# Routing a mixture of experts inside the attention before it, and streaming a later stage's logits

## The reference, cut to what matters

```python
t = t + _L2_attn_ref(_ln_t(t), Wq, Wk, Wv)            # causal attention, one head, 128 wide
t = t + _L2_ffn_ref(_ln_t(t), router_w, gate_w, up_w, down_w)
#   x = _ln_t(t);  router_logits = x @ router_w.T      # 16 experts
#   top_vals, top_idx = top_k(router_logits, 2);  weights = softmax(top_vals)
#   out = sum over the two of weights * ((silu(x @ gate) * (x @ up)) @ down)
...
t = t + _L3_ffn_ref(_ln_t(t), gate_weight, experts)
#   gate_logits = x @ gate_weight                      # 8 experts; then 8 rounds of Sinkhorn
```

## Time and profile before

| | |
|---|---|
| time, three runs | median 4058.59 us (4056.32 to 4060.82) |
| profiled execution | 4049.84 us, span 4048.0 us, mean granted TensorE clock 0.886 of full speed |
| busy: TensorE, VectorE, ScalarE, GpSimd | 83%, 76%, 46%, 27% of the span |
| attention | 1105 to 1332 us |
| routing | 1332 to 1560 us |
| logits of `sinkhorn_gates` | from 3789 us |

### The profile page before, as it was taken

How to read it: one execution, slowest core, us unless ns; L and a number is a source line. 1 busy time by engine, 2 the same in 40 slices (tenths; PEclk the granted TensorE clock), 3 DMA queues, 4 the chain that set the end, 5 groups by cost and what they waited for, 6 DMA issues and landing times. The chain is left out here.

```text
span 4048.0 us, 131348 instructions
## 1 busy us (share of the span) xinstructions
PE 3351.7 (83%) x54119; PEld 2132.4 (53%) x54119; DVE 3089.8 (76%) x7658; ACT 1857.2 (46%) x4392; POOL 1093.1 (27%) x1947
## 2 busy tenths in 40 slices
PE   5999999996699514996679999999679999998529
PEld 1333333222367412664357788877267788876414
DVE  7888788865766642556868999998868999997477
ACT  1666666673334101334456655554356655554200
POOL 1001001000000374551055544333056543332000
PEclk7999999998799656996579999999589999999659
DMA  6023233300000211224000000000000000000128
GB/s 145 24 48 54 39 54 54 54 8 6 0 1 1 87 51 50 67 69 156 1 9 15 9 9 9 9 4 6 4 8 15 9 9 9 9 4 9 47 74 302
DMA packets 102446, 155.92 MB, mean 39 GB/s; under 512 B 17060, under 2 KB 63017, under 8 KB 101824
## 3 DMA queue, kind: packets, MB, share of 16 engines
q1 hardware_dynamic: 87616, 120.28, 11.6%
q0 software_dynamic: 13088, 23.06, 2.0%
q10 hardware_dynamic: 1152, 4.19, 0.3%
HBM read 103.21 MB, written 45.30 MB: 37 GB/s over the span
## 5 line engine op out<-in xcount | busy, mean ns | idle before, releaser
L2079 ACT ACTIVATE s_E<-s_Y,s_M 128x9 f32<-128x9 f32 (+38 forms) x2048 | 656.6, 392 | 626.7 <-DVE s_M L1992 624.3
L365 DVE TENSOR_REDUCE half_max<-shared 128x1 f32<-128x512 f32 x1024 | 644.9, 684 | 89.0 <-PE shared L286 86.5
L1893 PE MATMUL g_x<-s_ik,s_iqm 128*32 128x1 f32 (+63 forms) x16384 | 676.4, 280 | 27.1 <-DVE g_o L1975 11.6
L482 ACT ACTIVATE E<-sc 128x1024 f32<-128x1024 f32 x512 | 496.7, 1021 | 268.8 <-PE sc L300 268.7
L1987 DVE SCALAR_TENSOR_TENSOR s_Y<-s_Y,g_x 128x9 f32<-128x9 f32 (+38 forms) x2048 | 578.7, 283 | 46.8 <-PE g_x L1893 1.2
L1905 PE MATMUL g_p<-mats,s_E 128*128 128x128 f32 x3072 | 448.1, 283 | 38.6 <-ACT s_E L2079 34.2
L1893 PEld LDWEIGHTS g_x<-s_ik,s_iqm 128*32 128x32 f32 x16384 | 395.1, 116 | 153.8 <-issue 79.4
L1905 PEld LDWEIGHTS g_p<-mats,s_E 128*128 128x128 f32 x3072 | 338.9, 144 | 104.4 <-ACT s_E L2079 60.4
L286 PE MATMUL shared<-ks,qs 96*128 96x512 bf16 x1024 | 373.5, 403 | 18.4 <-DVE half_max L365 13.3
L1992 DVE TENSOR_REDUCE s_M<-s_Y 128x4 f32<-128x8 f32 (+56 forms) x512 | 351.2, 686 | 0.8 <-DVE s_Y L1987 0.4
L2003 DVE TENSOR_TENSOR resid<-g_p,s_W 128x512 f32<-128x512 f32 x384 | 263.7, 687 | 59.7 <-PE g_p L1905 56.6
(11 more groups left out here) (353 smaller groups left out, 5227.2 us busy)
## 6 DMA issues: line engine op xcount, KB each, us to landing
e_spread<-d_gate SPq DMA_DIRECT2D x64, 512.0 KB, 6.1
d_parts<-parts SPq DMA_DIRECT2D x8, 1536.0 KB, 5.9
qs<-d_parts SPq DMA_DIRECT2D x96, 128.0 KB, 7.3
ks<-d_parts SPq DMA_DIRECT2D x96, 128.0 KB, 12.4
me_xg<-d_xs SPq DMA_DIRECT2D x144, 65.0 KB, 1.8
mc_yb<-d_ys SPq DMA_DIRECT2D x8, 1024.0 KB, 8.0
resid<-in_x SPq DMA_DIRECT2D x8, 512.0 KB, 8.2
rden<-d_den POOLq DMA_DIRECT2D x16, 256.0 KB, 3.7
```

The costliest lines, as they stand in the source:

```text
L365: dve.tensor_reduce(half_max[n // SETS % 2][:, idx // 2, idx % 2:idx % 2 + 1], bank("bm", n)[:, :], AX_X, ALU.max).then_inc(max_done, 1)
L482: act.activation(E[:, G % 2, h, :], sc[n % 2][:, :], ACT.Exp, scale=0.25).then_inc(exp_done, 1)
L1893: mm = pe.matmul(x_ps[u % 3][32 * b:32 * (b + 1), rho % 2, 0:n + 1], iqm[n // WINDOW % 2][:, b, x0:x0 + D, :], s.ik[:, b, rho, 0:n + 1], s ...
L2079: act.activation(E[:, m % 2, rho, 0:m + 1], Y[:, D * (m % YR) + rho, 1:2 + m], ACT.Exp, bias=M[:, D - 1 + D * m + rho:D + D * m + rho]).th ...
```

## The change

`layer2_attention` and `moe_route` become one block, `attend_and_route`. While batch r + 1 is attended, batch r is routed in pieces, each placed in a step; eight more steps without attention follow the 64 for batch 7.

- p0, p1 (`LOGITS`): TensorE makes the logits, half a batch each, straight from the residual; the router's weights are centred over the features once at the start, and since the deviation scales a token's 16 logits alike, the two best are the same. The difference of the best two is multiplied with 1/deviation later (`mark`).
- p1 (`BEST`): VectorE copies the logits out and takes the best.
- p2 and p4 (`FIRST`, `SECOND`): TensorE transposes half a batch in, VectorE takes the moments, ScalarE the root (Sqrt between the attention's Exp). In the steps behind them VectorE normalizes that half into `xt`.
- p3 (`INDEX`), p5 (`MARK`): VectorE's indices, then mask and running sum.
- p6 (`RANK`), p7 (`PLACE`): the two rank matmuls, then the positions. GpSimd scatters 16 times from there, as before.

The transposes back and ScalarE's copy of the normalized tokens are gone. Logits, transposed tokens and ranks share one PSUM bank; the even steps' scores get a half-size one. The weights' load starts with the attention; the zero rows are written by SP, with direct DMAs at 16 addresses loaded into registers, behind `padded`. The tables' large tensors lie in `t.xn`.

In `sinkhorn_gates` the gate's weights, padded to 32 columns, are the stationary operand and 512 tokens are streamed; four batches go to the four groups of 32 PSUM partitions. ScalarE and VectorE copy the rows out, 16 transposes bring the tokens back to the partitions, and the clip is done in two halves.

```diff
+                def logits(r, h):
+                    if h == 0:
+                        pe.wait_ge(added, NT * (r + 1))
+                        if r:
+                            pe.wait_ge(picked, r)
+                    for j in range(4 * h, 4 * h + 4):
+                        mm = pe.matmul(r_ps[:, j * NE:(j + 1) * NE], t.resid[:, r * T + j * P:r * T + (j + 1) * P],
+                                       centred[:, :], start=True, stop=True)
...
+                def tokens_in(r, h):
+                    if h == 0:
+                        pe.wait_ge(logit_done, r + 1)
+                    else:
+                        pe.wait_ge(normed, 2 * r + 1)
...
+                for g in range(STEPS + NT):
+                    r, p = g // NT - 1, g % NT
+                    if g < STEPS:
+                        turn(g, 0)
+                        if tile(g) >= HB:
+                            turn(g, 1)
+                        if g + 2 < STEPS:
+                            scores(g + 2)
+                        if piece(g):
+                            project(*piece(g))
+                    if r >= 0:
...
+                        if p in LOGITS:
+                            logits(r, p)
+                        if p == FIRST:
+                            tokens_in(r, 0)
+                        if p == SECOND:
+                            tokens_in(r, 1)
+                        if p == RANK:
+                            ranks(r)
+                    if g < STEPS:
+                        values(g)
...
+                    if r >= 0:
...
+                        if p == FIRST:
+                            moments(r, 0)
+                        if p == FIRST + 1:
+                            normalize(r, 0)
+                        if p == SECOND:
+                            moments(r, 1)
+                        if p == SECOND + 1:
+                            normalize(r, 1)
+                        if p == BEST:
+                            best(r)
+                        if p == INDEX:
+                            indices(r)
+                        if p == MARK:
+                            mark(r)
+                        if p == PLACE:
+                            place(r)
+                    if g < STEPS:
+                        finish(g)
...
+                for g in range(STEPS + NT):
+                    r, p = g // NT - 1, g % NT
+                    if g < STEPS:
+                        take_turned(g)
+                        if piece(g) and piece(g)[1] < 2:
+                            take_queries(*piece(g))
+                        if g + 2 < STEPS:
+                            exp(g + 2)
+                    if r >= 0 and p in (FIRST, SECOND):
+                        deviation(r, p == SECOND)
...
+                for r in range(2):
+                    for h in range(2):
+                        for q in range(4):
+                            c0 = (4 * r + q) * T + h * HALF
+                            mm_ = pe.matmul(rows_ps[32 * q:32 * q + 32, r, h * HALF:(h + 1) * HALF], f.gate_w[:, :],
+                                            t.xn[:, c0:c0 + HALF], start=True, stop=True)
```

More of the change, by code:

```diff
@@ new lines, in attend_and_route @@
+        logit = sb("logit", [P, NT, NE])
+        top = sb("top", [P, NT, 8])
+        index = sb("index", [P, NT, 8], U32)
+        indexf = [sb(f"indexf{i}", [P, 2, NT]) for i in range(2)]
+        gap = sb("gap", [P, NT])
+        diff = sb("diff", [P, B, NT])
+        mask = [sb(f"mask{i}", [P, NE, NQ + 1], BF16) for i in range(2)]
+        before = [sb(f"before{i}", [P, NE, NQ + 1], BF16) for i in range(2)]
+        chosen = sb("chosen", [P, NQ, NE])
+        rank = sb("rank", [P, NQ])
+        ones = sb("ones", [P, P], BF16)
@@ new lines, in attend_and_route @@
+        share = sb("share", [P, P])
+        centred = sb("centred", [P, NE])
+        lower = sb("lower", [P, P], BF16)
+        go_on = sb("go_on", [P, NE, NQ + 1], BF16)
+        iota_e = sb("iota_e", [P, NE])
+        iota_id = sb("iota_id", [P, NT])
+        iota_n = sb("iota_n", [P, TILES])
+        iota_r = sb("iota_r", [P, TILES])
+        iota_k = sb("iota_k", [P, N // P])
+        iota_pad = sb("iota_pad", [P, NE])
+        pad = sb("pad", [P, ROW])
+        count = sb("count", [P, NE])
@@ L926, in layer2_attention @@
+        pad_pos = sb("pad_pos", [P, NE], I32)
+        tiles = sb("tiles", [P, NE])
+        one_e = sb("one_e", [P, NE])
+        ends = sb("ends", [P, NE])
+        first = sb("first", [P, TILES])
+        full = t.xn[:, 0:NE * (N // P)].rearrange("p (e k) -> p e k", e=NE)
+        past = t.xn[:, T:T + TILES * NE].rearrange("p (n e) -> p n e", e=NE)
+        begun = t.xn[:, 4 * T:4 * T + TILES * NE].rearrange("p (n e) -> p n e", e=NE)
+        s_ps = [psum("s_ps0", HALF), psum("s_ps1", T)]
         t_ps = [psum(f"t_ps{i}", HALF) for i in range(2)]
+        x_ps = psum("x_ps", HALF)
@@ L1003, in values @@
                 def values(g):
[L1004 removed]
+                    b, n_tile = g // NT, tile(g)
                     if g % NT == 0:
@@ L1021, in _ @@
                 scores(1)
[L1022 to L1030, removed]
+                pe.wait_ge(m.router_in, 16)
+                pe.wait_ge(const, 4)
+                pe.matmul(r_ps[:, 0:NE], share[:, :], m.w_router[:, :], start=True, stop=True).then_inc(summed_w, 1)
+                for g in range(STEPS + NT):
[9 more added lines that the diff above has]
+                    if r >= 0:
+                        if r == 0 and p == 0:
+                            pe.wait_ge(centred_w, 1)
+                        if p in LOGITS:
[8 more added lines that the diff above has]
+                        values(g)
+                pe.wait_ge(picked, B)
+                pe.matmul(r_ps[:, 0:NE], ones[:, :], before[(B - 1) % 2][:, :, NQ], start=True, stop=True).then_inc(mm_n, 1)
             @block.vector
@@ L1059, in finish, with moments @@
                     dve.wait_ge(mm_o, g + 1)
-                    r = t.resid[:, c0:c0 + P]
-                    dve.tensor_tensor(r, o_ps[:, :], r, ALU.add).then_inc(added, 1)
+                    x = t.resid[:, c0:c0 + P]
+                    dve.tensor_tensor(x, o_ps[:, :], x, ALU.add).then_inc(added, 1)
+                def moments(r, h):
+                    k = 2 * r + h
+                    dve.wait_ge(token_in, k + 1)
+                    for j in range(4 * h, 4 * h + 4):
+                        bn = dve.bn_stats(stats[:, j, :], in_ps[:, (j - 4 * h) * P:(j - 4 * h + 1) * P])
+                    bn.then_inc(stat, 1)
+                    dve.wait_ge(stat, 2 * k + 1)
+                    if k:
+                        dve.wait_ge(root, k)
+                    for j in range(4 * h, 4 * h + 4):
+                        bn = dve.bn_aggr(mv[:, j, :], stats[:, j, :])
+                    bn.then_inc(stat, 1)
@@ new lines, in normalize @@
+                def normalize(r, h):
+                    k, i, four = 2 * r + h, r % RING, slice(4 * h, 4 * h + 4)
+                    dve.wait_ge(root, k + 1)
+                    dve.reciprocal(rstd[:, four], std[:, four]).then_inc(recip, 1)
+                    dve.wait_ge(recip, k + 1)
+                    if r >= RING:
+                        dve.wait_ge(sent[i], 16 * NQ * (r // RING))
+                    for j in range(4 * h, 4 * h + 4):
+                        ts = dve.tensor_scalar(xt[i][:, j, 0:P], in_ps[:, (j - 4 * h) * P:(j - 4 * h + 1) * P],
+                                               mv[:, j, 0:1], rstd[:, j:j + 1], ALU.subtract, ALU.mult)
+                    ts.then_inc(normed, 1)
@@ L1068, in _ @@
                 topmost(1)
-                scale(0)
-                for g in range(STEPS):
-                    if tile(g) >= HB:
-                        take_turned(g)
-                    if g + 1 < STEPS:
-                        scale(g + 1)
-                    if g + 2 < STEPS:
-                        topmost(g + 2)
-                    if piece(g) and piece(g)[1] >= 2:
-                        take_values(*piece(g))
-                    finish(g)
+                dve.wait_ge(summed_w, 1)
@@ new lines, in _ @@
+                dve.wait_ge(mm_n, 1)
+                dve.tensor_copy(count[:, :], r_ps[:, 0:NE]).then_inc(table, 1)
+                dve.wait_ge(table, 1)
+                dve.tensor_tensor(pad_pos[:, :], count[:, :], iota_pad[:, :], ALU.add).then_inc(padded, 1)
+                dve.tensor_tensor(full, count[:, :].unsqueeze(2).to_broadcast([P, NE, N // P]),
+                                  iota_k[:, :].unsqueeze(1).to_broadcast([P, NE, N // P]), ALU.is_gt).then_inc(table, 1)
+                dve.wait_ge(table, 2)
@@ new lines, in _ @@
+                dve.tensor_reduce(tiles[:, :], full, AX_X, ALU.add).then_inc(table, 1)
+                dve.wait_ge(table, 3)
+                dve.tensor_tensor_scan(ends[:, :], one_e[:, :], tiles[:, :], 0.0, ALU.mult, ALU.add).then_inc(table, 1)
+                dve.wait_ge(table, 4)
```

(16 more changed lines are left out.)

509 lines of the change are left out of this document (201 added, 308 removed).

## The result

The changed kernel took 3887.96 us (median of 4 runs, 3876.72 to 3893.91) beside 4057.45 us for the kernel before in the same session (4 runs, 4048.74 to 4060.82): a ratio of 0.9587, 95% interval [0.9561, 0.9612]. The forecast was 3918 in a range of 3880 to 3960. The profiled execution took 3886.5 us, 163.3 less than the one of before; the forecast for such a pair was 141.

The account below looks back on a forecast made before the run. The prediction took the attention as bound by TensorE and the routing by GpSimd's queue of 145 steps. Its terms, 183 - 55 - 1 + 14 = 141 us, taken from the median 4058.6, gave 3918 us, range 3880 to 3960.

Parts of the forecast that it names:

- (a): Routing stage: its own 224.2 us go, scatters ending 41.4 us behind the attention remain; gain 183 us.
- (b): Old routing stage: transposes back, ScalarE's copy and second buffer go, but were hidden under GpSimd; 0 beyond (a).
- (d): ScalarE in the attention: four function table loads a batch, 1.283 us each, hidden; 0, at most 36 us if uncovered.
- (c): Attention: routing pieces on VectorE and TensorE lengthen seven batches from 26.7 to 34.6 us; -55 us.
- the table: Routed attention: lengths forecast position by position, p0 to p7, from VectorE's and TensorE's work; sum 33.4 us a batch.
- The clock: Routed attention: TensorE gaps lower its clock, 3 us of work lost in every other batch, less slack; 1.2 us a batch.
- rival 1: Routed attention: VectorE runs almost without waits, batch 27.9 to 31 us; 3869 to 3892 us; chance 0.12.
- (e): Before the first attention step: one small matmul, centring and four memsets on the path; -1 us (0 to -2).
- (f): Last logits: streamed 512-column products and 16 transposes, 14.0 us against 28.2; +14 us, +18 at full clock.
- rival 2: Attention beside scatters: GpSimd and VectorE exclude each other, 12 to 54 us; 3930 to 3972 us; chance 0.13.
- Rival 3: Routed attention: in-order queues hide nothing, pieces add in full, 40.3 us a batch; 3958 us; chance 0.11.
- rival 4: Routed attention: TensorE's clock stays at the lower level, 58.4 us a batch; 4085 us; chance 0.04.

Follow-up runs that it names:

- run 10: The changed kernel with the 16 pad writes back on GpSimd behind the scatters; from last addition to GpSimd's last issue 63.0 us, before 42.5.
- run 11: The changed kernel with one operand of each of the three large table tensor_tensors in PSUM; from last addition to last scatter 38.9 us, 3.6 less.
- run 5: The changed kernel without ScalarE's square root, so without its table loads; attention stage 267.9 us beside 262.9, undisturbed batches 31.30 and 31.31.
- run 8: The changed kernel with the mark piece one position later (p6) and the ranks at p7; attention stage 250.5 us, 12.4 less.
- run 3: The changed kernel with the index piece's eight max_index operations done twice; p3 some 5.3 to some 6.4 us, attention stage 276.7 us.
- run 4: The changed kernel with each routing logits matmul done twice; p0 and p1 grew by 0.89 us each, the attention stage by 17.8 us.
- run 1: The kernel before with the streamed last logits alone; 4040.12 us beside 4055.94, ratio 0.9955.
- run 2: The changed kernel with eight row buffers and no scatter until all eight batches have positions; 4035.6 us, attention stage 264.9 us.
- run 9: The changed kernel with the first half of the logits not waiting for the batch's last addition; 0.30 us a batch less than 31.06.
- run 12: The changed kernel with mark late, early half of the logits and table operands in PSUM together; 3868.53 us, ratio 0.9555 to the kernel before.

## Why the prediction was right, and where its sizes were off

**(a) Right.** 224.2 - 42.5 = 181.7 us, forecast 183. The first scatter of batch 6 came 0.6 us before the last addition (forecast 1), batch 7's positions 14.3 us behind it (forecast 17), and the pads on SP's queue went by unseen: run 10 shows what they cost otherwise, 20.5 us. The tables' share in the tail, taken at 3.0 us, was 3.6 (run 11).

**(b) and (d).** For (d), run 5 takes away all loads, and an undisturbed batch is no shorter: right. (b) has no run of its own; that the sum below closes to 2 us with it at 0 speaks for it.

**(c) The mechanism was right, the term was mis-sized:** -55 us forecast, -35.7 measured. Three parts of it:
- The batch, 33.4 by the table, was 31.3 at full clock. p1 to p5 came within 0.4 us. p0 (3.6, measured 1.76) and p6 (2.7, measured 1.55) were too long: I added TensorE's pieces to the old length of steps in which TensorE had been idle (busy 1.23 of 2.74 and 1.85 of 2.35 us), and the idle time took the pieces up. In batch 1, whose p0 has the logits but follows a p7 without a place piece, p0 took 2.79 us, where it took 2.75 before. In the later batches the place piece delays the addition that ends p7; the exponential of 1024 columns, behind which ScalarE's copy for p0 stands, starts 1.33 us before the end of that addition instead of 0.16, and p0 is a further 1.0 us shorter. p7 (3.64, measured 4.8) was too short: the delay of p5 arrives there, as run 8 shows. Runs 3 and 4 confirm whose steps p3, p0 and p1 are.
- The clock, charged at 1.2 us a batch, was at the lower level in p1 of two of six batches, 1.69 us each: 0.56.
- The seventh batch was charged 7.9 us like the others and cost 4.3.
With six batches at 31.94 - 26.70 and one at 4.3 it is 35.7 us. The measured batch lies at the border that I had drawn between the forecast (31 to 38) and rival 1 (27.9 to 31), and the time, 3888, in rival 1's; but run 4 refutes rival 1's reason at p0 and p1, since 0.89 us more of TensorE costs 0.89 us there, and VectorE was not without waits: busy 26.95 of 31.31 us.

**(e) Right:** 0.6 us (18.9 to 19.5 until the first addition), forecast 1.

**(f) Mis-sized:** +20.1 us instead of +14, beyond the end that I gave, +18. I took 8.6 and 3.9 us for passes and transposes at the lower clock; they took 5.44 and 1.97. Of the 5.1 us between, some 3.3 are the clock, which rose in the middle of the passes: with the 0.85 us that a group of four took before the rise, all eight groups would have taken 6.8, and the transposes 3.9 (estimates). The other 1.8 are the price of a pass, which I had at 0.27 us for the lower level and which was 0.21. I had divided the busy time of the earlier trace rows; there the groups come in pairs, 0.45 us apart, and the time until the second has ended (612 ns a pass) is counted too. The last 1 us is mostly overlap, which I had left out: the first half's clip runs beside the second half's transposes. The end of +18 had the passes at the higher level, and not the transposes. Run 1 shows that the form does this by itself.

The sum, against the profiled executions: 181.7 - 35.7 - 0.6 + 20.1 = 165.5, and the stages around lost some 2 us; 163.3 were measured. The two mis-sized terms err to the same side, by 19 and 6 us, and no other term's error made up for them: the time lies 8 us inside the lower end of the range.

**The rivals.** What rival 2 feared is there and is small: with scatters beside it VectorE works up to 0.52 us longer a batch, and the batch is 0 to 0.24 longer (runs 2 and 10). In the changed kernel three of a batch's eight scale operations are longer than without scatters (352 to 538, 685 to 789 and 620 to 818 ns), the other five are not. The prediction had named longer scale operations as a sign that it is wrong; the sign came, with 0.5 us of them a batch instead of the 1.7 us and more that rival 2 needed. The Trainium skill, SBUF — State Buffer, section "Who interferes with whom", has two rules here. That VectorE with two inputs in SBUF contends with a GpSimd instruction that reads SBUF, and with one input there, outside a two-port mode, does not, run 11 agrees with: 1.91, 2.50 and 2.20 us with both, 0.97 with one in PSUM. The 2.50 us that the prediction set beside the second rule belong here, since a tensor_tensor ran beside that scatter. The second rule, that a two-port instruction and GpSimd block each other whole, these runs do not show at that size: at most 0.52 us in a batch with 16 scatters and eight scale operations. Rival 3 (40.3 us a batch) and rival 4 (clock low throughout; it was 0.95 over the stage) did not come. What rival 4 feared shows in single stretches: five at the lower clock in run 3 and seven in run 4, whose batches are longer. That the length of the batches brought them is not shown, since run 5, with the changed kernel's batch length, had five as well.

**What stays open.** Why the clock falls in some batches and not in others that have the same gaps: two stretches in the changed kernel, none in runs 8, 9 and 12, one to five in runs whose batches are as long as the changed kernel's (one in run 10, five in run 5), seven in run 4. In none of these runs was it made to fall or to stay.

## What to carry to other kernels

When a stage is put under another, go by positions and ask at each which engine sets the length; but add a piece to an engine's work there, not to the step's old length, or idle time is counted twice. A piece that makes one position late is paid again two positions on: moving it by one step (1.41 us a batch) was worth more than taking away either of the waits that it caused (0). A last batch, which prepares no next one, is charged apart.

## What the runs showed of the hardware

TensorE's clock stayed at the lower level (granted 0.50) through 27.5 us of back-to-back passes of 8 columns, and rose during 512-column passes in four column groups at the same place: in the fifth group of four in the changed kernel (0.85 us a group before, 0.43 after), in the sixth in run 1. The new form gained 20 us; at the lower level to the end it would have gained some 17 (an estimate from the 0.85 us a group and the 3.9 us for the transposes). Which property of the passes let the clock rise, no run separates. And a table operation's operand moved from SBUF to PSUM left the operation's own 2.55 us as they were, and gave the scatter beside it 1.5 us back (2.50 to 0.97).
